# Projecting q and k in pieces of 512 columns, with one piece of q or k and one of v per group, and normalising and squaring the batch rows tile by tile

## The reference, cut to what matters

```python
xn = layernorm(x)                                   # x: (8, 256, 512), over the last axis
q = einsum('oc,bct->bot', Wq, xn)  + bq             # (8, 256, 512)
k = einsum('oc,bcs->bos', Wk, ctx) + bk
v = einsum('oc,bcs->bos', Wv, ctx) + bv
dot = einsum('bhdt,bhds->bhts', q, k) / 4           # heads of 16 channels
dot = mask * dot - (1 - mask) * 1e6
out = einsum('bhts,bhds->bhdt', softmax(dot) * mask, v)
x = x + out
x = x + ffn(layernorm(x))                           # gates, top 2 of 8 experts, shared expert
```

## Time and profile before

| | us |
|---|---|
| median of 3 runs | 720.56 (720.54 to 720.6) |
| the profiled execution, its own time | 722.7 |
| its span, first to last instruction | 720.9 |
| PE busy | 629.1 (87%) |
| DVE busy | 516.7 (72%) |
| ACT busy | 449.4 (62%) |
| POOL busy | 321.6 (45%) |
| mean granted TensorE clock | 0.941 of full |

### The profile page before, as it was taken

How to read it: one execution, slowest core, us unless ns; L and a number is a source line. 1 busy time by engine, 2 the same in 40 slices (tenths; PEclk the granted TensorE clock), 3 DMA queues, 4 the chain that set the end, 5 groups by cost and what they waited for, 6 DMA issues and landing times.

```text
span 720.9 us, 11913 instructions
## 1 busy us (share of the span) xinstructions
PE 629.1 (87%) x3851; PEld 259.9 (36%) x3864; DVE 516.7 (72%) x959; ACT 449.4 (62%) x609; POOL 321.6 (45%) x444
## 2 busy tenths in 40 slices
PE   4888999999999999999999996778899899998960
PEld 3622332332333323323323321133454456665420
DVE  2497888888888888888888898743638444444684
ACT  3553877877877878877877876664432367774000
POOL 5584326346346355355443403331734544430664
PEclk9856999999999999999999997689999999999995
DMA  8543254364364354363334320041895233342454
GB/s 289 175 124 95 71 153 139 83 169 132 86 168 130 93 163 129 93 162 108 108 94 129 108 89 30 31 109 49 201 223 125 51 113 117 118 114 78 147 174 146
DMA packets 65611, 88.61 MB, mean 123 GB/s; under 512 B 12576, under 2 KB 46112, under 8 KB 64528
## 3 DMA queue, kind: packets, MB, share of 16 engines
q1 hardware_dynamic: 60992, 69.64, 32.1%
q0 software_dynamic: 4560, 18.22, 11.0%
HBM read 63.75 MB, written 32.74 MB: 134 GB/s over the span
## 4 chain that ended last, share of the span: by engine, by line
PE 66%; DVE 13%; ACT 8%; issue 6%; DMA 4%; POOL 2%; another core or an unknown queue 0%; SPq 0%; POOLq 0%; ACTq 0%; DVEq 0%
PE PS L859 16%; PE PS L831 10%; PE PS L640 8%; PE PS L766 8%; PE PS L1489 6%; ACT E L845 5%; DVE MX L772 5%; PE PS L719 4%; PE PS L1067 4%; PE PS L1550 3%; PE PS L1317 3%; DVE ST L393 2%; DMA E<-scr_ys,SL 2%; PE PS L1447 1%; ACT BIG L508 1%
## 5 line engine op out<-in xcount | busy, mean ns | idle before, releaser
L772 DVE TENSOR_REDUCE MX<-PS 128x1 f32<-128x512 f32 x512 | 326.7, 683 | 53.9 <-PE PS L766 53.3
L845 ACT ACTIVATE E<-PS 128x1024 f32<-128x1024 f32 x256 | 259.5, 1021 | 80.3 <-PE PS L831 79.5
L859 PE MATMUL PS<-E,BIG 128*32 128x512 f32 x1024 | 140.4, 621 | 3.3 <-ACT E L845 3.2
L766 PE MATMUL PS<-BIG 53*128 53x512 f16 x512 | 123.1, 400 | 17.5 <-DVE MX L772 17.2
L831 PE MATMUL PS<-BIG 55*128 55x512 f16 x512 | 103.1, 398 | 24.2 <-ACT E L845 20.7
L674 POOL TENSOR_TENSOR ML<-BIG,ML 128x512 f32<-128x512 f32 x30 | 38.3, 1277 | 142.6 <-ACT BIG L650 142.6
L831 PEld LDWEIGHTS PS<-BIG 55*128 55x128 f16 x512 | 24.7, 93 | 169.6 <-ACT E L845 99.7
L650 ACT ACTIVATE BIG<-PS,BIG 128x256 f32<-128x256 f32 x64 | 36.1, 565 | 36.1 <-PE PS L640 29.5
L1424 POOL DMA_INDIRECT CT<-scr_yr,IX x39 | 37.0, 949 | 43.9 <-PE PS L1447 36.9
L1511 DVE SCALAR_TENSOR_TENSOR E<-WP,PS 128x352 bf16<-128x352 f32 x39 | 20.3, 521 | 50.4 <-ACT WP L1501 46.7
L1489 PE MATMUL PS<-BIG,CT 128*128 x312 | 54.2, 318 | 0.6 <-issue 0.4
(11 more groups left out here) (211 smaller groups left out, 850.8 us busy)
## 6 DMA issues: line engine op xcount, KB each, us to landing
scr_parts<-WP SPq DMA_DIRECT2D x96, 128.0 KB
BIG<-scr_parts SPq DMA_DIRECT2D x64, 192.0 KB
BIG<-in_we POOLq DMA_DIRECT2D x8, 1088.0 KB, 14.1
scr_u<-ML SPq DMA_DIRECT2D x32, 256.0 KB, 2.1
scr_ys<-XN SPq DMA_DIRECT2D x19, 256.0 KB
X<-in_x SPq DMA_DIRECT2D x8, 512.0 KB, 6.3
CT<-in_ctx SPq DMA_DIRECT2D x8, 512.0 KB, 5.9
ML<-scr_u SPq DMA_DIRECT2D x16, 256.0 KB
```

The costliest lines, as they stand in the source:

```text
L766: e.matmul(PS[:, yi[name] % 3, :], QK[rows, qb(u), 0, j0 + jj, 128 * tt:128 * tt + 128], QK[rows, qb(u), 1, j0 + jj, :], start=True, stop= ...
L772: e.tensor_reduce(MX[:, g % 2, c:c + 1], PS[:, yi[name] % 3, :], AX.X, ALU.max)\
L845: e.activation(E[:, st, 2 * jj:2 * jj + 2, :], PS[:, slot(name):slot(name) + 2, :], ACT.Exp, scale=1 / 1024).then_inc(s["rc"], 1)
L859: ins = e.matmul(PS[32 * hh:32 * hh + 32, AVB, :], VT[:, b % 2, st, 4 * (g % 4) + hh, :], E[:, st, hh, :], start=(st == 0), stop=(st == 3))
```

## The change

1. q and k of a unit are one piece of 512 columns each (two matmuls of 512 columns, one evacuation of 512). The first matmul of q stands at position 2.55, between the x and the maxima of its step, the second at 2.75 behind the maxima; those of k at 6.55 and 6.75. Nothing of q or k stands at 3.75, 4.75 and 7.75 any more.
2. The second piece of v moves from position 2.75 to 4.75. Each group so has one piece of v and one of q or k.
3. For batches 2 to 7 the first of two bn_stats stands 4.2 IT ahead of the rest; the two normalisations stand 1.6 IT apart (3.2 and 4.8 instead of both at 2.4), and the two squares at 6.88 of the odd unit and 0.8 of the even one (both at 4.6 of the even one before).
4. The splits and the writes of q and k follow their pieces (0.6 and 1.9 IT behind the first matmul). The load of a batch's source follows the second piece of v, so it stands two IT later.

The diff, cut to its core:

```diff
-            ring += [(w - 3 + 3.75 * IT, ("q", w, 0)), (w - 3 + 4.75 * IT, ("q", w, 1)),
-                     (w - 3 + 6.75 * IT, ("k", w, 0)), (w - 3 + 7.75 * IT, ("k", w, 1))]
+            ring += [(w - 3 + (2.55 if w else 3.75) * IT, ("q", w)), (w - 3 + 6.55 * IT, ("k", w))]
             tv = -1 - .25 * IT if w == 1 else w - 2 + .75 * IT
-            mring += [(tv, ("v", w, 0)), (tv + (.1 if w == 1 else 2) * IT, ("v", w, 1))]
+            mring += [(tv, ("v", w, 0)), (tv + (.1 if w == 1 else 4) * IT, ("v", w, 1))]
...
+            def first_tile(e):
+                e.wait_ge(s_x[n], 16)
+                e.wait_ge(s["lnB"], n)
+                dch.step(e, e.bn_stats(ST6[:, 0, :], X[:, x0, :]))
...
-                for i in range(3 if n == 11 else 0, k):
+                for i in range(3 if n == 11 else 1 if 2 <= n < 8 else 0, k):
...
+            def normalise_one(i):
+                def f(e):
+                    e.wait_ge(s["lnB"], n + 1)
+                    e.wait_ge(s["rp"], zi["q", 2 * n - 3] + 1)
+                    ins = e.activation(XN[:, n % 2, i, :], X[:, x0 + i, :], ACT.Identity,
+                                       bias=NMR[:, n % 2, i:i + 1], scale=RR[:, n % 2, i:i + 1])
+                    if i:
+                        ins.then_inc(s["xn"], 1)
+                return f
...
+            if 2 <= n < 8:
+                dve.at(tA - .52, first_tile)
+                for i in range(2):
+                    act.at(tN + .2 * i, normalise_one(i))
+                return
...
-            act.at(-14 if b == 0 else when_at[name] - 1.2 * IT, squares)
+            for kt in range(2):
+                act.at(-14 if b == 0 else when_at[name] - 1.2 * IT if b == 1 else 2 * b - 4 + (-.14, .1)[kt], squares(kt))
...
+            name = ("qk"[i], w)
+
+            def mm(kt):
+                def f(e):
+                    if kt == 0:
+                        take_slot(e, name)
...
+                    src = XN[:, b % 2, kt, :] if i == 0 else CT[:, b % 2, kt, :]
+                    ins = e.matmul(PS[:, slot(name), :], WQ[:, i, kt, 128 * o:128 * o + 128], src,
+                                   start=(kt == 0), stop=(kt == 1))
+                    if kt:
+                        ins.then_inc(s["rp"], 1)
+                return f
+            for kt in range(2):
+                pe.at(when_at[name] + .2 * kt * IT, mm(kt))
...
+            act.at(when_at[name] + .2 * IT + DA, evac)
...
-            (pool if w else dve).at(when_at[name] + .4 * IT, split)
+            (pool if w else dve).at(when_at[name] + .6 * IT, split)
...
-            sp.at(when_at[name] + 1.7 * IT, write)
+            sp.at(when_at[name] + 1.9 * IT, write)
...
-            norm(b, 2 * b - 5 + .70, 2 * b - 5 + .75, 2 * b - 4 + .30)
+            norm(b, 2 * b - 5 + .70, 2 * b - 5 + .75, 2 * b - 4 + .40)
```

More of the change, by code:

```diff
@@ L426, in normalise @@
                         e.wait_ge(s["mp"], yi["v", 15, 1] + 1)
-                        e.wait_ge(s["rp"], zi["k", 15, 1] + 1)
+                        e.wait_ge(s["rp"], zi["k", 15] + 1)
                     else:
-                        e.wait_ge(s["rp"], zi["q", 15, 1] + 1)
+                        e.wait_ge(s["rp"], zi["q", 15] + 1)
                     dst = Y[n % 2]
@@ L501, in balance, with squares @@
             r8, bq, sk, bk = (COL[:, b % 2, 2 * i:2 * i + 2] for i in range(4))
[L503 to L507, removed]
+            def squares(kt):
+                def f(e):
+                    if kt == 0:
+                        e.wait_ge(s_ct[b % 2], 16 * (b // 2 + 1))
+                        if b >= 2:
+                            e.wait_ge(s["mp"], yi["f", b - 2] + 1)
                     ins = e.activation(SQ[:, kt, :], CT[:, b % 2, kt, :], ACT.Square,
                                        accum_out=SQA[:, b % 2, kt:kt + 1])
-                ins.then_inc(s["sqa"], 1)
-            act.at(-14 if b == 0 else when_at[name] - 1.2 * IT, squares)
+                    if kt:
+                        ins.then_inc(s["sqa"], 1)
+                return f
+            for kt in range(2):
+                act.at(-14 if b == 0 else when_at[name] - 1.2 * IT if b == 1 else 2 * b - 4 + (-.14, .1)[kt], squares(kt))
             def mm(e):
@@ L637, in mm, with evac @@
                             e.wait_ge(s["w1"], 16) if i else e.wait_ge(s["w"], 32)
[L638 to L655, removed]
+                    src = XN[:, b % 2, kt, :] if i == 0 else CT[:, b % 2, kt, :]
+                    ins = e.matmul(PS[:, slot(name), :], WQ[:, i, kt, 128 * o:128 * o + 128], src,
+                                   start=(kt == 0), stop=(kt == 1))
+                    if kt:
+                        ins.then_inc(s["rp"], 1)
+                return f
+            for kt in range(2):
+                pe.at(when_at[name] + .2 * kt * IT, mm(kt))
+            def evac(e):
+                e.wait_ge(s["rp"], zi[name] + 1)
+                e.wait_ge(s["bal"], b + 1)
+                if w:
+                    e.wait_ge(s["fr%d" % i], w)
+                e.activation(FB[:, i, :], PS[:, slot(name), :], ACT.Identity,
+                             bias=COL[:, b % 2, 4 * i + 2 + o:4 * i + 3 + o],
+                             scale=COL[:, b % 2, 4 * i + o:4 * i + o + 1]).then_inc(s["rc"], 1)
+            act.at(when_at[name] + .2 * IT + DA, evac)
         def split_part(w, i):
             b = w // 2
-            name = ("qk"[i], w, 1)
+            name = ("qk"[i], w)
             chain = pch if w else dch
```

10 lines of the change are left out of this document (4 added, 6 removed).

## The result

| | before | after |
|---|---|---|
| median of 4 runs, us | 720.58 (720.54 to 721.38) | 765.03 (761.63 to 766.8) |
| the profiled execution, its span | 720.9 | 762.4 |
| start until the first exponential | 64.9 | 65.2 |
| from there to the start of unit 14 | 367.0 | 408.5 |
| from there to the end | 289.1 | 288.8 |

The changed kernel is slower: ratio 1.061, 95% interval 1.057 to 1.065. The forecast of 728.9 had the sign and less than a fifth of the size (+44.5 against +8.3), and the time lies outside the range of 717 to 735.

What follows compares the result with a forecast made beforehand. The prediction took PE to fill each half, with DVE's bank release causing waits at the empty step. Terms 15.1 - 6.0 - 2.0 + 1.2 = +8.3 on 720.56 gave 728.9 us; the range leaving out 2 in 10 was 717 to 735.

Steps and rivals of the forecast that it cites:

- the piece: PE's q or k matmuls: four records of 512 columns take 1.94 (1.76 to 2.12), the step holding them 2.56.
- the empty step: At 3.75 and 7.75 PE waits for DVE to free banks: 0.94 per half; half +0.58, +15.1 us over 26.
- POOL's split and the writes start earlier, which costs nothing either: Splits and writes of q and k: moving them earlier adds 0, since parts are loaded about a unit before use.
- Records back to back at 0.44: PE's 512-column records of q or k: a sign of being wrong, where the forecast expected 0.48 to 0.49 each.
- Squares, -6.0: ACT in six even units: setting squares apart leaves some 0.26 of 1.26 batch work; -6.0 us, range 0 to -7.6.
- Statistics, -2.0 in the odd units: DVE in five odd units: one bn_stats moves to a step that ACT bounds; -2.0 us, range 0 to -4.5.
- the source, +1.2: Batch source load in five odd units: landing later, it may delay the square by 0.25 each; +1.2 us.
- rival D: Source load lands at 8 instead of 6.2, each odd unit loses 1.8 more: +9, about 738 us; chance 0.03.
- Start and feed-forward part, 0: Kernel's start 0, range -2 to +2; feed-forward part untouched, 0, though its clock phases may shift by 1 or 2 us.
- A: Rival on the empty step: DVE keeps up, waits stay at 0.25 per half; faster, 710.9 us; chance 0.15.
- B: Rival of no change: piece costs 1.76, waits 0.75, half 12.89; 719.3 to 722 us; chance 0.11.
- C: Clock rival: waits bring 1.2 GHz stretches in one of two of 13 units; 11 on top, about 740; chance 0.06.

Runs made afterwards that it cites:

- h_adj: a_nolock with both matmuls of a q or k piece in a row behind the maxima, at 2.75 and 6.75: 739.25 us, ratio 1.024.
- a_nolock: The changed kernel with one added wait per split: POOL starts splitting q or k only after DVE's two small tiles of negated maxima: 746.41 us, ratio 1.035.
- b_lock: The kernel before, with an added POOL instruction on a scratch tensor beside DVE's small write of negated maxima, groups 2 to 27: 730.25 us, ratio 1.013.
- g_v: a_nolock with the v pieces at 3.75 and 7.75, so 0.75 and 4.75 are empty, and the squares in one place again: 764.12 us, ratio 1.057.
- f_nobatch: The changed kernel with statistics, normalisations and squares back at their old places: 773.07 us, ratio 1.072.
- s_sq: The kernel before with only the squares set apart, from batch 3 on, and the small product f at 2.8 instead of 5.8: 717.15 us, ratio 0.993.
- d_best: s_sq with the changed kernel's edits to statistics and normalisations too, from batch 3 on: 713.07 us, ratio 0.987.

## Why the prediction was wrong

Four kernels in a row split the plain unit: 25.36 before, 26.64 in h_adj, 27.24 in a_nolock, 28.98 after. The forecast was 26.52. Step by step on PE the miss of 2.46 per unit is 1.90 for the meeting of DVE and POOL (2 x 0.95), 0.40 for the piece (2 x (2.76 - 2.56)) and 0.14 for the waits at the empty step (2 x (1.01 - 0.94)), 2.44 in sum.

- **The step that failed** is the sentence "POOL's split and the writes start earlier, which costs nothing either". The split moved beside DVE's small write of the negated maxima and blocks it for 0.95, once per group. It costs 1.90 per unit, of which a_nolock gives back 28.98 - 27.24 = 1.74; in the medians that is 18.6 us (765.03 to 746.41), over half of the miss of 36. b_lock shows the same delay with nothing else of the change. Unit 13, which the forecast left alone, is longer as well (24.85): the split of the last k meets L804 there once, for 0.95, and its two pieces of v now both stand behind empty steps, where each waits the 0.37 that the prediction itself had found; 0.95 + 0.74 is 1.69, measured 1.61.
- **The piece** was mis-sized. It was taken at 1.94, and is 1.92 when its matmuls stand in a row (h_adj), but 2.12 as it stands in the changed kernel. The step with the piece is 2.45 there and 2.76 after; the forecast had 2.56, with one change of weights for the splitting and nothing else. The splitting costs 27.24 - 26.64 = 0.60 per unit, 7.8 us in 13 units. Of the 0.31 per step that this is, the prediction had 0.09. The 0.045 that the earlier trace rows showed per record is not a price of the record but of a group (below), and the splitting makes two groups of one. So the 1.94 came near the 1.92 by luck: too much per record and nothing per group. Records back to back at 0.44, which the prediction had named as a sign of being wrong, are there (0.43), and the time they save is lost again by the splitting.
- **The empty step** was right in its mechanism. The waits were forecast at 0.94 per half, 0.64 + 0.37 by one way of working, and h_adj and the changed kernel show those two numbers. The unit of h_adj is 1.28 longer than before; 2 x 0.58 = 1.16 was forecast, for a step with the piece that was 0.11 longer than it is in h_adj. In the medians h_adj is 16.9 us longer (739.25 against 722.39), but that holds its other parts too and is no measure of the +15.1 alone. g_v shows that the 0.64 goes with the empty step and not with its neighbours.
- **Squares, -6.0:** even units fell from 1.26 of batch work to 0.46, which gives -4.8 in six of them. But f_nobatch shows 0.47 with the old places too. The mechanism (2.60 between two exponentials) was right for the kernel before (s_sq, -0.94 per even unit), and in the changed kernel the other parts of the change had already covered it.
- **Statistics, -2.0 in the odd units, and the source, +1.2:** odd units went from 0.90 to 0.75 over the plain one, -0.7 in five. The source landed in 4.5 to 5.4 (5.8 to 6.3 before) and no square waited for it, so the +1.2 and rival D are gone. Without part 3 the odd units 5, 7 and 9 would have been 3.04 over the plain one (f_nobatch), so that edit was worth 2.3 in each, over five times what was forecast. The 1.01 that the earlier trace rows show is idle time of the weight loads; the matmul behind them waited 0.52.
- **Start and feed-forward part, 0:** right (65.2 against 64.9, 288.8 against 289.1).
- **The rivals.** A and B fell with the waits of 1.01. C fell as well: the granted clock from unit 0 to unit 13 is 0.99 in both kernels. None of the rivals held a meeting of DVE and POOL.

The account of the profiled executions, from the first exponential to unit 14: 13 units at 3.62 are +47.1; batch work -4.8 and -0.7; unit 13 +1.6; and unit 3 of the kernel before had a stretch at the lower clock, which the changed one lacks, -1.6. The sum is +41.6, measured +41.5.

For h_adj the work of a half is 6.12 + 1.60 + 1.51 + 2.45 + 0.53 = 12.21, and with 1.01 of waits the unit would be 26.44. The measured 26.64 is 0.20 more, and 0.17 of that is one step of the second half (1.70 instead of 1.53), behind the product of the reciprocals, which POOL's split holds up here too (0.76).

What stays open: why unit 0 runs partly at 1.2 GHz in some executions was not tried. The gain and the loss of the edits per batch in the changed kernel are told from the spacing of the exponentials; no run moved squares, normalisations or statistics one by one there.

## What to carry to other kernels

When work moves on POOL, look at which DVE instructions it will stand beside: a small one like L804 (a tensor_scalar from SBUF to SBUF), L785 or L924 (two inputs in SBUF) ended only when POOL's did, here up to 2.5 us later than alone, and what is queued behind it pays. Look for one such row in the trace of before, however rare, since it gives the price. And a step emptied of matmuls isn't free while PSUM banks tie PE to DVE: fill steps evenly, or set only the slow extra work apart, which here gave 1.3% (d_best, with f moved too). Where a change splits a run of f32 matmuls around others, count what each new group costs.

## What the runs showed of the hardware

- A DVE tensor_scalar of 128x16 took 0.17 alone and 1.13 beside POOL (after), 0.82 where POOL had begun earlier (b_lock), and ended 0.02 to 0.03 after POOL's instruction. A tensor_tensor of 128x32 with two inputs in SBUF took 0.75 instead of 0.19 (a_nolock) and ended 0.05 after it. Reductions from PSUM stayed at 0.68 and a reciprocal at 0.34 beside the same POOL instructions.
- An f32 matmul with 128 weight columns stands in the profile as two records. Four records of 512 columns in a row take 1.92 (h_adj) and two take 1.06 (after), so a record is (1.92 - 1.06) / 2 = 0.43, about two of the f16 passes of 0.22, and each group of such matmuls has 1.06 - 0.86 = 0.20 on top. With half of that per record, 0.215, a 256-column piece comes out as 4 x 0.215 + 0.20 = 1.06, which is what the earlier trace rows show.
